# First SAGE sweep begun ahead of the last count sweep; second home for features, new batch order, zone width and load depth

## What is computed

```python
x = _layernorm(x + _L0(x, ...))   # three GCN layers with edge weights, then Wl
x = _layernorm(x + _L1(x, ...))   # two SAGE layers:
    #   h = relu(x @ W1_self + mean_neighbours(x) @ W1_neigh + b1)
    #   out = h @ W2_self + mean_neighbours(h) @ W2_neigh + b2
x = _layernorm(x + _L2(x, ...))   # encoder, five GRU steps with conv_w, decoder
x = _layernorm(x + _L3(x, ...))   # one GCN layer on edge counts
```

## Time and profile before

| | us |
|---|---|
| median of 3 runs | 5418.55 (5417.47 to 5427.17) |
| the profiled execution | 5422.52 |
| its span, first to last instruction | 5420.8 |
| PE busy in the span | 4761.6 (88%) |
| POOL busy in the span | 2487.1 (46%), all of it but some 30 us before 3050 |
| DVE, ACT busy | 1668.7 and 1430.4 |

### The profile page before, as it was taken

How to read it: one execution, slowest core, us unless ns; L and a number is a source line. 1 busy time by engine, 2 the same in 40 slices (tenths; PEclk the granted TensorE clock), 3 DMA queues, 4 the chain that set the end, 5 groups by cost and what they waited for, 6 DMA issues and landing times.

```text
span 5420.8 us, 76798 instructions
## 1 busy us (share of the span) xinstructions
PE 4761.6 (88%) x25659; PEld 2555.4 (47%) x25659; DVE 1668.7 (31%) x3023; ACT 1430.4 (26%) x2732; POOL 2487.1 (46%) x1708
## 2 busy tenths in 40 slices
PE   3555555899939999999999599999999999999999
PEld 3555555444414445444455244544444444444444
DVE  9999999200001000110051201402113021120642
ACT  7899999100011111111120000302112021120320
POOL 4788888878887888888888400000000000000000
PEclk7555655899969999999999799999999999999999
DMA  9999994799859999999999587696775867768477
GB/s 351 370 366 340 338 331 85 209 332 297 230 133 306 280 300 300 280 279 299 255 257 266 129 298 242 187 299 199 245 257 181 288 198 257 245 194 287 155 233 249
DMA packets 717693, 1402.42 MB, mean 259 GB/s; under 512 B 268948, under 2 KB 363112, under 8 KB 686184
## 3 DMA queue, kind: packets, MB, share of 16 engines
q1 hardware_dynamic: 477388, 1342.89, 74.2%
q0 software_dynamic: 225792, 0.70, 7.9%
q10 hardware_dynamic: 14364, 56.99, 2.8%
HBM read 1160.09 MB, written 240.26 MB: 258 GB/s over the span
## 4 chain that ended last, share of the span: by engine, by line
PE 42%; POOL 38%; issue 10%; DMA 1%; POOLq 1%; DVE 0%; SPq 0%; ACT 0%; ACTq 0%; DVEq 0%
PE psum L969 34%; POOL C_adj L601 21%; POOL W_adj L601 16%; PE psum L920 2%; PE psum L922 2%; PE psum L927 1%; PE psum L924 1%; POOLq L595 1%; PE psum L952 0%; DMA W_adj<-arena 0%; POOL arena L575 0%; DMA C_adj<-arena 0%; POOLq L357 0%; PE psum L900 0%; PE psum L1041 0%
## 5 line engine op out<-in xcount | busy, mean ns | idle before, releaser
L969 PE MATMUL psum<-arena 128*128 128x512 f16 (+3 forms) x14014 | 3676.2, 422 | 147.7 <-issue 88.8
L969 PEld LDWEIGHTS psum<-arena 128*128 (+2 forms) x14014 | 1670.2, 123 | 2098.1 <-issue 978.1
L601 POOL DMA_INDIRECT W_adj<-arena x784 | 1215.0, 1550 | 277.1 <-issue 252.4
L601 POOL DMA_INDIRECT C_adj<-arena x784 | 1217.7, 1553 | 242.4 <-issue 242.4
L802 POOL TENSOR_TENSOR arena<-arena 128x512 f32 (+1 forms) x13 | 21.8, 1677 | 1692.5 <-DVE arena L1483 1692.5
L549 PE MATMUL psum<-arena 128*128 (+1 forms) x6664 | 223.4, 167 | 428.7 <-DVE arena L495 408.0
L469 DVE TENSOR_SCALAR_CACHE_REDUCE arena<-arena 128x2048 bf16<-128x2048 f32 (+5 forms) x294 | 572.0, 2007 | 0.0
L301 ACT ACTIVATE arena<-arena 128x1280 bf16<-128x1280 f32 (+4 forms) x490 | 426.7, 880 | 88.5 <-PE psum L555 35.3
L309 ACT ACTIVATE arena<-arena 128x1280 bf16<-128x1280 bf16 (+4 forms) x490 | 424.3, 866 | 0.0
L549 PEld LDWEIGHTS psum<-arena 128*128 128x128 bf16 x6664 | 213.3, 104 | 441.2 <-issue 395.4
L1724 DVE COPY arena<-psum 128x512 f32<-128x512 f32 (+1 forms) x39 | 23.2, 653 | 1220.8 <-PE psum L1008 849.5
(11 more groups left out here) (264 smaller groups left out, 2578.9 us busy)
## 6 DMA issues: line engine op xcount, KB each, us to landing
arena<-C_adj SPq DMA_DIRECT2D x686, 384.0 KB
arena<-C_adj SPq DMA_DIRECT2D x441, 512.0 KB
arena<-W_adj SPq DMA_DIRECT2D x196, 1024.0 KB
arena<-W_adj SPq DMA_DIRECT2D x196, 768.0 KB
arena<-C_adj SPq DMA_DIRECT2D x343, 288.0 KB
W_adj<-arena SPq DMA_DIRECT2D x12, 6400.0 KB
W_adj<-arena SPq DMA_DIRECT2D x12, 6144.0 KB
arena<-W_adj SPq DMA_DIRECT2D x98, 576.0 KB
```

The lines of the kernel that those rows point to most:

```text
L601: return pool.indirect_dma_start(table, bass.IndirectOffsetOnAxis(idx[:, t:t + 1], 0), values[:, of:of + 1], None, compute_op=ALU.add)
L969: ins = pe.matmul(psum[:, bank + b, 0:width], lhs, ring[:, slot, b * BANK:b * BANK + width], start=begin and part == 0, stop=False, skip_g ...
```

## The change

1. `SAGE_PART`: the first 33 chunks (of 49) of stage sage's first sweep are loaded and multiplied in front of gcn 2's last sweep. They take blocks 5 to 8 and source chunks 4 to 36, whose units 1 to 9 are ready by then.
2. Split features get a second home: two regions `side[0]`, `side[1]` take turns, unit by unit with both parts side by side, so the SAGE features can be written while gcn 2's are still read. `two_parts` of a SAGE unit moves from stage sage into `sage_unit`.
3. Units 1 to 4 use two sets of banks and two output buffers in turn, and PE takes the next unit's products before the turning of the one before.
4. Stage sage's sweeps become blocks (5..8), (9..12), (2..4), (0..1) in place of (0..3), (4..6), (7..9), (10..12).
5. `ORDER` changes so that no neighbours share target nodes. From the first on: before 48 46 47 45 43 41 44 42 39 37 ..., now 48 46 44 47 45 42 40 43 41 38 ...
6. `W_adj` is zeroed in zones of 256 columns (25) in place of 512 (13); `C_adj` as before. In both cases the zones of `W_adj` go down from the 128-wide one.
7. Load c waits for load c-3 in all four sweeps of stage start.

```diff
+ZONE = 256
+ZONE_COUNT = -(-NP // ZONE)
...
-ORDER = [0] + [4 * g + u for g in range((NB - 5) // 4) for u in (2, 4, 1, 3)]
-ORDER += [b for u in (0, 1) for b in range(len(ORDER) + u, NB - 1, 2)] + [NB - 1]
-ORDER = ORDER[::-1]
+ORDER = [NB - 1] + [t - d for t in range(NB - 2, 8, -4) for d in (1, 3, 0, 2)] + [7, 5, 2, 4, 1, 6, 3, 0]
...
-SAGE_BANKS = ((0, 1, 2), (4, 5, 6), (5, 6, 7), (5, 6, 7))
+SAGE_BANKS = (((0, 1, 2),), ((4, 5, 6),), ((5, 6, 7), (0, 1, 2)), ((5, 6, 7),))
+SAGE_LAPS = 4
+SAGE_PART = 1 + SAGE_LAPS * LAP
+SAGE_SWEEPS = ((5, 4, 0), (9, 4, 4), (2, 3, 0), (0, 2, 4))
...
-        for table, of, zeroed in ((W_rows, zero, w_zeroed), (C_rows, z16, c_zeroed)):
-            for done, z in enumerate(reversed(range(BLOCKS))):
-                at_, width = z * BANK, block_width(z)
+        for table, of, zeroed, zone in ((W_rows, zero, w_zeroed, ZONE), (C_rows, z16, c_zeroed, BANK)):
+            for done, at_ in enumerate(reversed(range(0, NP, zone))):
+                width = min(zone, NP - at_)
...
-    h_parts = take(P, [2, PAD * P], F16)
-    sum_fm = take(P, [PAD * P], F32)
+    side = [take(P, [PAD * P], F32) for _ in range(2)]
+    h_nm = side[0].rearrange("p (c f) -> p c f", f=D)
+    halves = [r.bitcast(F16).rearrange("p (u t x) -> p u t x", u=UNITS, t=2) for r in side]
...
+                if added and (name, sweep) == ("gcn", SPLIT):
+                    e0, columns = SAGE_SWEEPS[0][0] * BANK, SAGE_SWEEPS[0][1] * BANK
+                    for place in range(SAGE_PART):
+                        slot = LAP if place == 0 else (place - 1) % LAP
+                        if place:
+                            sp.wait_ge(s["chunk_used"], used + place - LAP + 1)
+                        sp.dma_start(ring[:, slot, 0:columns], table[ds(sage_chunk(place) * P, P), e0:e0 + columns]) \
+                            .then_inc(landed[slot], 16)
...
-                first_sweep = k == 0 and sweep == 0
-                for c in range(1, CHUNKS if first_sweep else 1):
+                if k == 0:
+                    laps = LAPS * sweep
+                    for c in range(1, CHUNKS):
...
+                        if c > 2:
+                            sp.wait_ge(landed[(c - 3) % LAP], 16 * (laps + (c - 3) // LAP + 1))
...
-                        for j in sage_units_of(sweep - 1):
-                            sage_products(j, sweep - 1, ahead)
-                            sage_turned(j, sweep - 1, ahead, before)
+                        units = sage_units_of(sweep - 1)
+                        for i_, j in enumerate(units):
+                            sage_products(j, ahead, 2 if i_ else 1)
+                            if i_:
+                                sage_turned(units[i_ - 1], ahead, before, 2 if i_ > 1 else 1)
+                        sage_turned(units[-1], ahead, before, 2)
+                        pe.wait_ge(s["seconds_read"], ahead.seconds + sage_units().index(units[-1]) + 1)
+                        for place in range(SAGE_PART):
+                            sage_spell(place, ahead)
...
-                dve.tensor_scalar(sum_nodes(j), work, 0.0, None, ALU.max).then_inc(s["unit_set"], 1)
+                dve.tensor_scalar(out_nodes(n), work, 0.0, None, ALU.max).then_inc(s["unit_set"], 1)
                 dve.wait_ge(s["unit_set"], before + n + 1)
+                two_parts(out_nodes(n), j, up[:, 0:1], ahead.features + n + 1, parts_of(SAGE_STAGE))
```

More of the change, by code:

```diff
@@ L639, in sage_units_of, with sage_banks @@
     return range(first, first + n)
-def sage_splits():
-    return [j for j in range(UNITS) if j not in sage_units_of(SPLIT)] + list(sage_units_of(SPLIT))
+def sage_banks(j):
+    sweep = next(i for i in range(len(DOWNWARD)) if j in sage_units_of(i))
+    return SAGE_BANKS[sweep][j % len(SAGE_BANKS[sweep])]
 def sage_chunk(place):
@@ L774, in nodes, with summed, sums_to, parts_of @@
         return ap[:, ds(j * UC, UC), :]
-    def sum_nodes(j):
-        return unit(sum_fm, j).rearrange("p (c f) -> p c f", f=D)
+    def summed(k):
+        return side[1] if k <= SAGE_STAGE else side[0]
+    def sums_to(k):
+        return side[1] if k < SAGE_STAGE else side[0]
+    def parts_of(k):
+        return halves[0] if k < SAGE_STAGE else halves[1]
+    def half(parts, part, j):
+        return parts[:, ds(j, 1), part, :].rearrange("p a x -> p (a x)")
+    def out_nodes(n):
+        return unit_out[:, n % 2]
     def bank_nm(b):
@@ L838, in sync @@
                 if (name, sweep) == ("sage", 0):
[L839 to L848, removed]
+                    for place in range(SAGE_PART, CHUNKS):
+                        sp.wait_ge(s["chunk_used"], used + place - SAGE_PART + 1 - LAP + 1)
+                        load(sage_chunk(place), (place - 1) % LAP)
+                    used += CHUNKS - SAGE_PART
                     continue
                 load(0, LAP)
-                first_sweep = k == 0 and sweep == 0
-                for c in range(1, CHUNKS if first_sweep else 1):
[L853 to L860, removed]
+                if k == 0:
+                    laps = LAPS * sweep
+                    for c in range(1, CHUNKS):
+                        slot, lap = (c - 1) % LAP, laps + (c - 1) // LAP
+                        sp.wait_ge(s["chunk_used"], used + c - LAP + 1)
+                        if c == 2:
+                            sp.wait_ge(landed[LAP], 16 * (sweep + 1))
+                        if c > 2:
+                            sp.wait_ge(landed[(c - 3) % LAP], 16 * (laps + (c - 3) // LAP + 1))
+                        load(c, slot)
                     used += CHUNKS
@@ L967, in chunk @@
                         width = block_width(first + b)
-                        lhs = chunk32[:, slot32, :] if wide else h_parts[:, part, ds(c * P, P)]
+                        lhs = chunk32[:, slot32, :] if wide else half(held, part, u_)[:, w_ * P:(w_ + 1) * P]
                         ins = pe.matmul(psum[:, bank + b, 0:width], lhs, ring[:, slot, b * BANK:b * BANK + width],
@@ L971, in chunk, with sage_products @@
                 ins.then_inc(s["chunk_used"], 1)
-            def sage_products(j, sweep, ahead):
+            def sage_products(j, ahead, behind=1):
                 n = sage_units().index(j)
-                pe.wait_ge(s["products_read"], ahead.read + n)
-                near, own, _ = SAGE_BANKS[sweep]
+                pe.wait_ge(s["products_read"], ahead.read + n + 1 - behind)
+                near, own, _ = sage_banks(j)
                 for c in range(UC):
@@ L1146, in tensor @@
                             else:
[L1147 removed]
+                                sage_turned(units[lap - 1], ahead, before)
                             if j is not None:
[L1149 removed]
+                                sage_products(j, ahead)
                             lap += 1
@@ L1508, in two_parts, with sage_unit @@
                                          op1=ALU.subtract).then_inc(s["features_set"], 1)
-                dve.wait_ge(s["features_set"], (j if n is None else n) + (base.features + 1))
-            def sage_unit(j, sweep, ahead, before):
+                dve.wait_ge(s["features_set"], j + (base.features + 1) if done is None else done)
+            def sage_unit(j, ahead, before):
                 n = sage_units().index(j)
+                dve.wait_ge(s["seconds"], ahead.seconds + max(n - 1, 0))
                 dve.wait_ge(s["products"], ahead.products + n + 1)
-                near, own, _ = (bank_nm(b) for b in SAGE_BANKS[sweep])
+                near, own, _ = (bank_nm(b) for b in sage_banks(j))
                 for c in range(UC):
```

143 lines of the change are left out of this document (73 added, 70 removed).

## The result

The changed kernel takes 5386.77 us (median of 4 runs, 5383.77 to 5392.81) against 5421.99 for the kernel before, measured beside it: ratio 0.9936, 95% interval 0.9919 to 0.9953. That is 35 us faster where 58.5 were forecast, and 3.8 us above the range of 5343 to 5383. Its profiled span is 5385.5 us, 35.3 less than before.

A forecast was written before the change was run, and what follows sets the result against it. It took POOL's adds to bound the kernel up to about 3050 and PE's matmuls after. Terms -48 - 4 - 8 + 1.5 = -58.5 took the profiled 5422.5 to 5364, as a median 5360; range 5343 to 5383.

The forecast's parts named there:

- Term 4, its price: Stage start's last sweep: holding its 256 KB loads makes PE wait, +1.5 us, ends 0 and +6.
- Term 4, its gain: Stage start: holding loads in all four sweeps takes 8 of POOL's 11.6 us stall before 1155.77, ends 0 and -11.6.
- Term 3: POOL's first batches: narrower zones and new order start the third batch at 143.9 in place of 147.84, -4 us.
- rival A: Zeroing `W_adj`: short lines are free, third batch at 133.8, gain there 14 us, kernel 5350; chance 0.15.
- Terms 1 and 2: Units 1 to 4 through SAGE's first sweep: moved chunks fill PE's 38.21 us wait, units overlap; -48 together, units about -6.
- The cover: Before gcn 2's last sweep: POOL's adds end 20 us before PE needs them, so nobody waits.
- At nothing: Changes expected to gain nothing, such as the count side's 13.93 us conflict wait going, since nobody waits for POOL's end.
- B: Stage start: adds stay crowded, POOL's stall returns elsewhere and held 256 KB loads cost the full 6, 5372; chance 0.15.
- E: Zeroing `W_adj`: a zone costs by its lines, not bytes, so batch 44 starts 90 us late, 5454; chance 0.03.

The follow-up runs named there:

- e2: The changed kernel with three loads in flight in place of two in all four sweeps of stage start: 5364.52 us.
- e1: The changed kernel with the hold on loads taken off stage start's last sweep alone: 5354.48 us.
- e3: The changed kernel with loads held in the first sweep of stage start alone, as before the change: 5366.13 us.
- e7: The kernel of e1 with `W_adj` zeroed in zones of 512 columns as before the change, new batch order kept: 5366.42 us.
- e6: The kernel of e1 with the batch order of before the change: 5346.73 us.
- e8: The kernel of e1 with SP's loads of gcn 2's last sweep written out in place of a loop of eight: 5351.77 us.
- e5: The kernel of e1 with 9 chunks in front of gcn 2's last sweep in place of 33: 5369.51 us.
- e10: The kernel of e1 with units 1 to 4 again strictly in turn and in one set of banks: 5359.87 us.
- e11: The kernel of e1 unchanged, run once more: 5351.16 us.

## Why the prediction was wrong, point by point

- **Term 4, its price (+1.5, ends 0 and +6): measured +25.7.** This is the step that failed, and alone it takes 5360 to 5384. Two errors met. The code holds two loads in flight, I read three: with three the sweep takes 53.4 us (e2), 8.3 over before, and the kernel 5364.5, inside the range; the misreading cost the other 17.4. And I took PE's waits in 1000 to 1480 as the bound. All 6.3 us lie before 1145, in the one sweep that was held, and its loads are of 832 KB. There PE works 2.8 us on a chunk, so two in flight hide a trip of 5.6 us. A chunk of 256 KB is 0.87 us of PE work and two hide 1.7, while the trip is 2.7 to 3. The row that bore on it was the last sweep's own, 98 matmuls in 45.23 us, set against the time of one load, and not a sum of waits for larger ones. PE's timeline in the held sweep of the changed kernel, ten chunks of eight matmuls:

```profile
1102.39 28.24 PE L994 MATMUL psum<-arena 128*128 128x512 f32 x80 [1.12 <-DMA arena<-W_adj]
```

- **Term 4, its gain (-8, ends 0 and -11.6): -4.0 in the profiled execution**, about -9 in most of the held kernels, and -11.7 by the medians of e1 against e3. The size was about right, the reasoning was not: I took the stall for a mark of sweep 1's beginning, but it comes every 112 adds whatever the loads do, and a shorter one stays when they are held.
- **Term 3 (-4): -8.5.** The zone's price was right over the whole table, 22.6 against 22.9, but the four zones that the third batch waits for came in 86.1 us, 21.5 each (53.2 to 139.35). The third batch at 139.35 lies halfway between my 144 and rival A's 134. Short lines are not free: in the same stretch zones of 512 columns take 40.7 (e7), half of which is 20.4; but they cost 5 to 8% more, not the 10% that I took from the count table. The first batch waited for its cells at 58.6 as said. That the new order eats the gain was right and more: e6 shows 6.2 us.
- **Terms 1 and 2 (-48): -47.7.** First product to first moved chunk 17.5 us; part and last sweep 89.8 to the end of the sweep against 87.5. The last sweep is SP's (e8), the gap comes back when the part is cut (e5), units 7.8 (e10). The cover was more than the 20 us said: the last count add is issued at 3021.2, and the part's 33 chunks of 1.73 us last until about 3076. The low end of the range adds up to -37 and not to the -38 given (last sweep 6.2 longer, units 5.3).
- **At nothing:** the count side's conflict wait is hidden (e6). The longer zeroing delayed nothing: its last count zone is issued at 828.7 (before, 787.8), and PE ends the first weight sweep at 1136.8 (before, 1136.6).
- **The rivals.** B named the held 256 KB loads as a price but capped it at 6, from the same wrong row. E's mechanism, a zone priced by its lines, is refuted by 22.6. The sign of the change was right, and so was the place of its gain, the filled wait; the size was 0.6 of the forecast. -47.7, -8.5, -4.0 and +25.7 add up to -34.5 of the -35.3 in span. The forecast was counted from 5418.55, and the kernel before took 3.4 us more beside the changed one; by the ratio alone 5418.55 becomes 5383.9, at the edge of the range.

## What to carry to other kernels

When a wait limits the loads in flight, divide one load's whole round trip by their number and compare it with the consumer's time a load, for each size of load under the limit and not for the largest alone. Count them from the slot that the wait names. A limit that costs next to nothing in a sweep of 832 KB or 1 MB loads can hold up the sweep of 256 KB loads behind it, and that one may stand right behind the longest wait of the kernel.

A wait for another engine is best filled with later work whose inputs are ready, and its worth is the length of the wait. Once it is filled with time to spare, a delay on the awaited engine costs nothing as long as it stays within that cover (here some 50 us), and reordering work to spare that engine is worth nothing either.

Before you explain a stall by what begins at the same moment, look for the same stall elsewhere in the trace and count instructions between them.

## What the runs showed of the hardware that was not expected

- A 256 KB load into SBUF with nothing else of its queue in flight takes 2.70 us from one chunk to the next; with two in flight 2.9, with three 3.3 for each.
- POOL pauses after every 112 of its indirect weight adds, in all fourteen traces, before the 450th alone not. The pause is 0.7 to 11.6 us long; the one near 1140 was 1.85 to 7.60 us in executions that hold the loads of sweep 1, and 2.16 and 5.13 in two executions of one kernel (e1, e11). No run here shows its cause.
- SP issues loads with constant addresses at 0.56 us each (e8) where the loop of eight took 0.655.
